# Narrower work on the diagonal pairs of a causal attention in a two-layer decoder kernel

## The reference, cut to what matters

```python
def _L0_xattn_ref(query, key_value, Wq, bq, Wk, bk, Wv, bv, Wo, bo):
    ...
    scores = jnp.einsum('bhqd,bhkd->bhqk', Q, K) / np.sqrt(HEAD_DIM)
    causal = jnp.tril(jnp.ones((SQ, SKV), bool))
    scores = jnp.where(causal[None, None], scores, -jnp.inf)
    attn = jax.nn.softmax(scores, axis=-1)
    out = jnp.einsum('bhqk,bhkd->bhqd', attn, V)
```

## Time and profile before

| | |
|---|---|
| median of 3 runs | 3341.07 us (3337.25 to 3341.98) |
| profiled execution | 3343.19 us, its span 3341.4 us |
| busy of the span | PE 2966.9 us (89%), DVE 2076.8 us (62%), ACT 1604.4 us (48%) |
| mean granted TensorE clock | 0.939 of full speed |
| the changed stage | first scores at 547.9 us, last times V from 1030.3 us |
| instructions in it | 592 score and 208 mask products, 1184 records of times V, 296 exps, 578 maxima |

### The profile page before, as it was taken

How to read it: one execution, slowest core, us unless ns; L and a number is a source line. 1 busy time by engine, 2 the same in 40 slices (tenths; PEclk the granted TensorE clock), 3 DMA queues, 4 the chain that set the end, 5 groups by cost and what they waited for, 6 DMA issues and landing times. The chain is left out here.

```text
span 3341.4 us, 45425 instructions
## 1 busy us (share of the span) xinstructions
PE 2966.9 (89%) x15822; PEld 1295.8 (39%) x15823; DVE 2076.8 (62%) x4240; ACT 1604.4 (48%) x2122; POOL 225.1 (7%) x295
## 2 busy tenths in 40 slices
PE   6586978999997898799999999999999999559993
PEld 3364552333334455133333333333333332336662
DVE  4334137777774234778888888888888887312224
ACT  2123313655664222256666666666666667313331
POOL 3002100000001001210000000000000000030003
PEclk9788988999999899699999999999999999779996
DMA  5412032011000002412121112111111110430012
GB/s 152 108 39 89 0 100 74 1 35 36 1 1 2 34 0 78 121 40 58 30 58 48 34 48 53 29 38 51 41 41 41 41 41 21 166 116 31 31 34 83
DMA packets 112721, 171.00 MB, mean 51 GB/s; under 512 B 17882, under 2 KB 88427, under 8 KB 112147
## 3 DMA queue, kind: packets, MB, share of 16 engines
q1 hardware_dynamic: 109460, 160.11, 17.1%
q0 software_dynamic: 3072, 8.39, 0.8%
HBM read 127.63 MB, written 40.51 MB: 50 GB/s over the span
## 5 line engine op out<-in xcount | busy, mean ns | idle before, releaser
L1283 DVE TENSOR_REDUCE d_part_max<-d_ps_m 128x1 f32<-128x512 f32 (+1 forms) x1964 | 1131.3, 631 | 165.8 <-PE d_ps_m L1271 147.4
L1589 ACT ACTIVATE d_prob<-d_ps_s 128x1024 f32<-128x1024 f32 x928 | 899.4, 1021 | 407.9 <-PE d_ps_s L1459 400.4
L1271 PE MATMUL d_ps_m<-k_st,q_st 97*128 97x512 bf16 (+1 forms) x1324 | 469.0, 363 | 20.5 <-DVE d_part_max L1283 16.7
L1459 PE MATMUL d_ps_s<-q_st,k_st 98*128 98x512 bf16 x1276 | 428.2, 382 | 6.1 <-ACT d_prob L1589 4.2
L679 DVE TENSOR_REDUCE x_part_max<-x_att_ps_m 128x1 f32<-128x512 f32 (+2 forms) x578 | 318.5, 588 | 113.1 <-PE x_att_ps_m L658 60.8
L917 ACT ACTIVATE x_att_prob<-x_att_ps_s 128x1024 f32<-128x1024 f32 x296 | 291.4, 1022 | 178.2 <-PE x_att_ps_s L801 89.5
L1271 PEld LDWEIGHTS d_ps_m<-k_st,q_st 97*128 97x128 bf16 x1324 | 125.5, 97 | 427.5 <-DVE d_part_max L1283 318.8
L1476 PE MATMUL d_ps_o<-d_prob,a_values 128*32 128x512 f32 x2048 | 273.6, 606 | 0.0
L1271 PE MATMUL d_ps_m<-q_st 97*128 97x512 bf16 (+1 forms) x640 | 226.2, 363 | 2.4 <-DVE d_part_max L1283 0.7
L1476 PE MATMUL d_ps_o<-d_prob,x_values 128*32 128x512 f32 x1664 | 221.7, 604 | 0.4 <-ACT d_prob L1589 0.4
L801 PE MATMUL x_att_ps_s<-q_st,k_st 98*128 98x512 bf16 x592 | 206.7, 382 | 3.4 <-ACT x_att_prob L917 1.8
(11 more groups left out here) (326 smaller groups left out, 3238.0 us busy)
## 6 DMA issues: line engine op xcount, KB each, us to landing
k_st<-parts_k SPq DMA_DIRECT2D x90, 256.0 KB, 5.7
k_st<-parts_k SPq DMA_DIRECT2D x90, 208.0 KB, 4.7
l_w<-in_l_w SPq DMA_DIRECT2D x16, 1024.0 KB, 11.6
q_st<-parts_q SPq DMA_DIRECT2D x48, 256.0 KB, 4.8
q_st<-parts_q SPq DMA_DIRECT2D x192, 64.0 KB
q_st<-parts_k SPq DMA_DIRECT2D x30, 256.0 KB
q_st<-parts_k SPq DMA_DIRECT2D x30, 208.0 KB
parts_q<-a_proj_parts SPq DMA_DIRECT2D x16, 384.0 KB, 2.5
```

The lines of the kernel that those rows point to most:

```text
L1271: pe.matmul(bank[:, 0:w], self.query(s, h, ROW_MASK + 1, a * P, P), self.key(s, h, ROW_MASK + 1, k, w), start=True, stop=True).then_inc(s_ ...
L1283: dve.tensor_reduce(self.part[:, h * QT + a, i:i + 1], bank[:, 0:w], AX.X, ALU.max).then_inc(s_read, 1)
L1459: mm = pe.matmul(ps_s[u][:, hh, :], maxima.key(s, h, ROW_MAX + 1, kt * P, P), maxima.query(s, h, ROW_MAX + 1, 0, QC), start=True, stop=True)
L1589: act.activation(prob[:, p % 2, 2 * u:2 * u + 2, :], ps_s[u][:, :, :], ACT.Exp, scale=scale).then_inc(s_prob, 1)
```

## The change

On a diagonal pair at position d, nothing is computed for the first q0 = 128 d queries of the chunk, since none of them may see this key tile. Scores, exp and times V take queries q0 to 511 alone. The mask product then covers only the 128 queries at q0, where the diagonal itself runs, with one 128x128 table; the queries behind it see the whole tile and need no mask. The first key tile of every chunk still has q0 = 0 or lies before the diagonal, so each column of `ps_o` is begun by a full product. Nothing is moved: the number and order of instructions on each engine are the same as before. The band form and the second layer's attentions are untouched.

```diff
+    def first_query(self, c, kt):
+        return max(kt - QT * c, 0) * P if self.kind == "causal" else 0
...
-    c["causal_k"] = sb("causal_k", [P, 2 * QC], BF16)
+    c["causal_k"] = sb("causal_k", [P, P], BF16)
...
-            select(c["causal_k"][:, :], ALU.is_ge, NEG, -off, [[1, 2 * QC]], -1)
+            select(c["causal_k"][:, :], ALU.is_ge, NEG, 0, [[1, P]], -1)
...
-                        diag = at.kind == "causal" and kt >= QT * c
-                        mm = pe.matmul(bank[:, hh, :],
+                        q0 = at.first_query(c, kt)
+                        mm = pe.matmul(bank[:, hh, q0:QC],
                                        k_st[0:ROW_MAX + 1, bass.ds(slot(g), 1), h, kt * P:(kt + 1) * P],
-                                       q_st[0:ROW_MAX + 1, bass.ds(slot(g), 1), h, c * QC:(c + 1) * QC],
-                                       start=True, stop=not diag)
-                        if diag:
-                            off = QC - P - P * (kt - QT * c)
-                            mm = pe.matmul(bank[:, hh, :], cst["ident_bf"][:, :],
-                                           cst["causal_k"][:, off:off + QC], start=False, stop=True)
+                                       q_st[0:ROW_MAX + 1, bass.ds(slot(g), 1), h, c * QC + q0:(c + 1) * QC],
+                                       start=True, stop=True)
+                        if at.kind == "causal" and kt >= QT * c:
+                            mm = pe.matmul(bank[:, hh, q0:q0 + P], cst["ident_bf"][:, :], cst["causal_k"][:, :],
+                                           start=False, stop=True, skip_group_check=True)
...
+                    q0 = at.first_query(c, kt)
                     for j in range(GH):
-                        mm = pe.matmul(ps_o[32 * j:32 * j + 32, :], v_grp[:, kt, j, :], prob[:, k % 2, j, :],
+                        mm = pe.matmul(ps_o[32 * j:32 * j + 32, q0:QC], v_grp[:, kt, j, :],
+                                       prob[:, k % 2, j, q0:QC],
                                        start=(i == 0), stop=(i == n - 1), skip_group_check=True)
...
-                            act.activation(prob[:, k % 2, 2 * u:2 * u + 2, :], bank[:, :, :], ACT.Exp,
+                            q0 = at.first_query(c, at.key_tiles(c)[i])
+                            act.activation(prob[:, k % 2, 2 * u:2 * u + 2, q0:QC], bank[:, :, q0:QC], ACT.Exp,
                                            scale=scale).then_inc(s_prob, 1)
```

## The result

| | median us | runs |
|---|---|---|
| before | 3341.53 (3337.25 to 3343.48) | 4 |
| changed | 3289.95 (3286.44 to 3296.06) | 4 |

The ratio is 0.9849 [0.9832, 0.9867]. Predicted was 3284, a gain of 57.

A forecast was written before the change was run, and what follows sets the result against it. PE was taken to bound the attention stage, except where ACT paces group 3's last chunk. Gross 64.6 us minus 4.9, 2.2, 0.5 and 0.2 gave 57 us: 3284 us, range 3275 to 3299.

The forecast's parts named there:

- rival 2: On PE, narrow products cost more than their columns: gain 51 us, 3290 us; chance 0.12.
- The signs that the prediction named: Stage 425 us instead of 482 to the last times V; wrong if PE waits for L679 or L917 exceed 15.
- Masks: On PE, 208 mask products go from 512 to 128 columns, saving 33.3 us.
- Prices of narrow scores and times V: On PE, narrow products cost by width: scores save 15.0 us, times V 15.4 us.
- DVE, predicted 0.5 us: Maxima at position 3 of chunk 1 and the next pair slightly outlast PE; three banks carry over: 0.5 us lost.
- Rival 1: DVE or ACT becomes the diagonal's bound: DVE form costs 20 us, 3304; ACT form 3293; chance 0.16 in either form.
- The row of maxima in groups 0 to 2: Before chunk 3's scores, PE waits for the maxima's DMA chain: 0.9 us a group, 2.6 us in all.
- Group 3, predicted 2.5: In group 3, 2.3 us lost at the row of maxima and DVE's last maxima, 0.2 in ACT's stretch.
- ACT, predicted 2.2: At chunk and group starts PE waits for exps: 0.16 us nine times, 0.24 at three group starts, 2.2 us.
- POOL's shorter table: At kernel start, fill and select shrink but SP waits for x_tok anyway: costed at nothing, two us at most.
- Rival 3: Granted clock falls to half inside the stage because PE meets new waits: 131 us more, 3415 us; chance 0.03.
- the allowance of 6 us: Behind the stage, an earlier start may meet the granted clock better or worse: 6 us either side.

The follow-up runs named there:

- f1: Changed kernel with the causal form's maxima taken over the first half of their columns only: 3272.55 us, ratio 0.9804.
- f0: The changed kernel measured again, unedited, beside other experiments on the same chip: 3288.59 us, ratio 0.9848.
- e1: Changed kernel with scores, exps and times V over all 512 queries again, only the masks narrow: 3307.15 us, ratio 0.9910.
- second record: Second recorded execution (trace) of the unedited changed kernel: stage 431.3 us, 2309.7 us behind it.
- f3: Changed kernel, turn of the maxima two entries behind the last maximum instead of four, due 2.0 pairs ahead, 2.5 in group 3: 3279.97 us, ratio 0.9827.
- e3: Changed kernel with exps over all 512 queries again, all else narrow: 3289.09 us, ratio 0.9847.
- e4: Changed kernel with the causal form's maxima due 2.5 pairs before their chunk instead of 1.5: 3289.68 us, ratio 0.9845.
- g1: Kernel before the change with the earlier-turn edits of f3: 3336.92 us against 3337.64, ratio 1.0000.
- h1: f3 with DVE's groups 1 and 2 written out instead of a two-round loop: 3279.45 us, ratio 0.9826.
- f2: Changed kernel, turn two entries behind the last maximum instead of four, due 2.0 pairs ahead, group 3 left at 1.5: 3283.43 us, ratio 0.9831.
- g2: f3 with maxima spread by weight, fewer on diagonal pairs, due 1.5 pairs ahead, 2.0 in group 3: 3285.76 us, ratio 0.9850.
- e2: Changed kernel with exps and times V over all 512 queries again, masks and scores narrow: 3296.97 us, ratio 0.9869.

## Why the prediction was right, and where it was not

The range and the mechanism held: PE was the bound, and what its columns cost could be read from starts. The time alone does not say so: 3290 us is just what rival 2 gave. What speaks against that rival are the starts in the trace, and f1, which gets part of the missing gain back without touching PE. The signs that the prediction named came out so: the stage to the start of its last times V took 431.9 and 430.3 us, where 425 was said; PE's waits for DVE and ACT that have rows of their own are 3.6 us in f0, far from 15; the part behind the stage was 6.0 us longer in one record, at the edge of what was allowed, and not in the other. By its steps:

- **Masks, 33.3 us (34.1 with the half-clock start): right.** e1 gave 33.0 by the medians, 32.3 in the stage.
- **Prices of narrow scores and times V: right.** The earlier trace rows gave 0.058 us for a narrow product and 0.79, 0.57 and 0.36 us for times V, and so did the trace after (0.785, 0.572 and 0.358 as medians). The dearer 128-column product (81 ns in the Trainium skill, TensorE: Matmul & The Clock Gate, back-to-back issue gap) does not appear: this trace disagrees with 58 to 60 ns.
- **But these two terms did not arrive whole:** 15.0 became 8.3, and 15.4 became 10.8 in the stage. The sum of what was taken back is 12.5 us (64.6 - 52.1, second record), where 7.8 was predicted. That is the gap between 57 and the 52 of that record.
- **DVE, predicted 0.5 us: the mis-sized term.** I looked for places where DVE's mean pace (0.534 us a maximum) is slower than PE and found one. What counts is that three banks carry over only a short burst: two or three entries in a row between the now shorter pieces wait some tenths each (0.60 us for 0.44). f1 gives back 0.94, 1.06, 1.06 and 1.08 us in chunks 0 and 1 of the four groups, 4.1 us together; the columns there say 3.8. All of f1's gain in the stage, 7.0, is the upper end; the part of it in chunks 2 and 3 the kernel before may have given away too, and no run of it with shorter maxima was made. Rival 1 (20 us, a maximum holding its bank for all of 0.69 us) was far too strong, since a group lost 1 us and not 5.
- **The loop border, not predicted.** PE waits 0.96 us at the border of groups 1 and 2, since DVE stands still for 2.5 us there. Its price is less than the wait: chunk 3 of group 1 takes 41.35 us (41.17 in the second record), that of groups 0 and 2 40.9, so 0.4 and 0.25 us. DVE stood still in the trace before too (2.42 us), where chunk 3 of groups 0 and 1 took the same 42.8, and I did not look at what was hidden behind PE.
- **The row of maxima in groups 0 to 2, 0.9 us each: right,** 0.92. (That is from the last start before the wait, 725.40, plus its product's price of 0.115, to the scores at 726.43; the profile's row counts 0.75, since products overlap.) Group 1, chunk by chunk (first record): its columns are worth 52 x 0.160 + 12 x 0.313 + 3 x 1.28 = 15.9 us, it gained 13.0, and of the 2.9 us between 1.06 are in chunks 0 and 1, 1.17 in chunk 2 (the row and 0.25 more), 0.67 in chunk 3 (the border and 0.25 more).
- **Group 3, predicted 2.5 (2.3 and 0.2): too low.** Columns behind its first times V are worth 14.4 us and 9.7 came (f0). About 1.1 of the rest is the ring. The other 3.7 are 3.4 in chunk 2, about the late turn (0.76 us behind DVE's last maxima), the row (1.73) and the exps behind it, and 0.3 in chunk 3, where ACT sets the pace; f3, with an earlier turn, gets 2.0 back. How the rest divides between row and exps was not separated.
- **ACT, predicted 2.2: too high.** Groups 0 to 2 gained 40.5 of 3 x 15.9 = 47.7 us. Of the 7.2 missing, 2.8 are the row, 2.8 the ring in chunks 0 and 1 and 0.4 the border. Some 1.2 us are left for ACT and all else. e3 shows that longer exps on diagonal pairs cost nothing; the full exps of a new chunk, which the term was about, no run changed.
- **POOL's shorter table: nothing, as said.** Its last select ended at 16.05 us instead of 17.08, and SP still waited 6.4 us for x_tok:

```profile
15.11 0.94 POOL L175 TENSOR_SCALAR_AFFINE_SELECT band_q<-band_q 128x256 bf16<-128x256 bf16 x2
```

```profile
SPq L148 <- DMA x_tok<-in_x: 6.4, 1, 6.4
```

- **Clock.** Rival 3 in its strong form did not happen. A weak form did: one stretch of some 7 us behind a 1.7 us wait, in some executions, for 2.2 us. Behind the stage the allowance of 6 us was just used up: 2316.1 us in the first record, 2309.7 in the second, 2310.1 before.

## What to carry to other kernels

When an engine without idle time gets shorter pieces, price them by the distance between starts, and then go through every burst of the engine that follows it: its mean pace says little where only a few buffers carry a burst over. Chains with a fixed latency (here turn, copy, four DMAs, 4.1 to 4.7 us) need their lead in time, not in steps; when steps become shorter the lead must grow, but without packing more of the follower's work in front. Groups 0 to 2 show both: a lead of 2.5 pairs cost on the diagonal what it saved behind it (e4), and one of 2.0 pairs with a shorter tail saved the wait (f3). And give the remedy to the old kernel as well (g1): a part of what it brings may have been there before the change.

## What was unexpected of the hardware

- DVE stands still for 2.4 to 2.7 us between two rounds of a loop whose body is one group, in every version with the loop, and not when the rounds are written out (h1). It waits for no data there. Its sequencer ends the loop's branch at 797.08 us in the trace before and has its next instruction at 799.92, 2.84 us later (2.8 to 3.1 in all versions with the loop); what it does in between no run shows. The row before names PE as releaser, but the product that its first maximum reads had its last start at 797.22:

```profile
800.04 3.01 DVE L679 TENSOR_REDUCE x_part_max<-x_att_ps_m 128x1 f32<-128x128 f32 x6 [2.42 <-PE x_att_ps_m L658]
```

- The same kernel with the same 1.73 us wait of PE fell to half clock behind it in one recorded execution and not in another. Such stretches of 3.4 to 6.8 us lie inside the stage in five kernels (the changed kernel 947.9 to 954.7, e3 949.1 to 952.6, f2 940.7 to 944.1, e4 773.8 to 777.2, g2 766.2 to 773.0 us), and in the records of before, f0, e1, e2, f1, f3, g1 and h1 there is none. f0 and f1 have the wait as well.
